# Keeping the conv blocks and silu(z) in HBM, with a lag of 20 blocks, new instruction orders, and the layer norms' squares on ScalarE

## What is computed

```
xz = x @ W_in                      # 256 -> 2 x 512: x_proj, z
x_conv = silu(conv4(x_proj) + conv_b)          # causal, 4 taps, per channel
ssm = x_conv @ W_xproj                         # 33 columns: delta, B (16), C (16)
h_mean = einsum('bld,bln->bdn', x_conv, softplus(delta) * B) / L     # over the whole sequence
y = einsum('bdn,bln->bld', h_mean, C) + D * x_conv
x = layernorm(x + (y * silu(z)) @ W_out)
gate, up = fp4_linear(x, w_gate), fp4_linear(x, w_up)                # 256 -> 704 each
x = layernorm(x + fp4_linear(silu(gate) * up, w_down))               # 704 -> 256
```

## Time and profile before

| | |
|---|---|
| median of three executions | 2203.39 us |
| the profiled execution: its own time | 2204.03 us |
| span of its trace, first to last instruction | 2202.1 us |
| mean granted TensorE clock | 0.98 |
| TensorE busy | 1990.6 us, 90% |
| VectorE busy | 1756.7 us, 80% |
| ScalarE busy | 1111.5 us, 50% |
| GpSimd busy | 1115.6 us, 51% |
| DMA | 90.53 MB, mean 41 GB/s |

### The profile page before, as it was taken

How to read it: one execution, slowest core, us unless ns; L and a number is a source line. 1 busy time by engine, 2 the same in 40 slices (tenths; PEclk the granted TensorE clock), 3 DMA queues, 4 the chain that set the end, 5 groups by cost and what they waited for, 6 DMA issues and landing times.

```text
span 2202.1 us, 37847 instructions
## 1 busy us (share of the span) xinstructions
PE 1990.6 (90%) x10532; PEld 1583.8 (72%) x10532; DVE 1756.7 (80%) x3548; ACT 1111.5 (50%) x2100; POOL 1115.6 (51%) x1643
## 2 busy tenths in 40 slices
PE   1887899899999999899999999899999999877776
PEld 1655688688877888688877888688876888666665
DVE  6234788798978888789877888798887888788875
ACT  2665455555545555455544556455544555423332
POOL 2223455466545556455644555465554556445543
PEclk9999999999999999999999999999999999999998
DMA  2111111111111111111111111111111111000000
GB/s 79 50 56 43 34 49 44 44 43 45 49 41 34 44 48 45 36 49 49 41 38 41 44 44 48 38 49 44 39 41 39 49 45 35 29 20 25 20 20 15
DMA packets 77089, 90.53 MB, mean 41 GB/s; under 512 B 8881, under 2 KB 59953, under 8 KB 76849
## 3 DMA queue, kind: packets, MB, share of 16 engines
q1 hardware_dynamic: 76848, 87.73, 12.2%
HBM read 37.37 MB, written 16.78 MB: 25 GB/s over the span
## 4 chain that ended last, share of the span: by engine, by line
PE 76%; issue 5%; DVE 4%; ACT 3%; POOL 1%; ACTq 0%; DVEq 0%; POOLq 0%
PE pgu L489 23%; PE pd L489 14%; PE pd L537 9%; PE pa L489 6%; PE pb L489 6%; PE pc L571 4%; PE pc L519 4%; PE pe_ L631 2%; PE pa L559 2%; PE pc L496 2%; PE pe_ L548 1%; PE pd L638 1%; DVE hbuf L990 1%; DVE qsh L820 1%; PE pa L615 1%
## 5 line engine op out<-in xcount | busy, mean ns | idle before, releaser
L489 PE MATMUL pgu<-wgu_hi,xqT 128*128 128x512 f32 (+1 forms) x1536 | 427.7, 387 | 0.9 <-issue 0.9
L489 PE MATMUL pd<-wd_hi,hqT 128*128 128x256 f32 (+1 forms) x1536 | 334.5, 299 | 18.7 <-DVE r L1012 15.5
L489 PEld LDWEIGHTS pgu<-wgu_hi,xqT 128*128 128x128 f32 x1536 | 279.8, 190 | 75.8 <-issue 27.6
L537 PE MATMUL pd<-wout,g 128*128 128x256 f32 x1024 | 259.9, 398 | 49.6 <-DVE hqT L980 35.2
L489 PEld LDWEIGHTS pd<-wd_hi,hqT 128*128 128x128 f32 (+1 forms) x1536 | 255.8, 190 | 57.4 <-issue 23.8
L946 DVE SCALAR_TENSOR_TENSOR acc<-xps,cw,acc 128x512 f32<-128x512 f32 x256 | 248.7, 972 | 24.4 <-POOL acc L429 23.7
L418 POOL TENSOR_SCALAR rs<-mv 128x1 f32<-128x1 f32 x128 | 61.6, 481 | 396.4 <-DVE mv L1027 228.8
L537 PEld LDWEIGHTS pd<-wout,g 128*128 128x128 f32 x1024 | 191.5, 195 | 79.7 <-issue 56.0
L741 ACT ACTIVATE hqT<-pe_ 128x512 fp32r<-128x512 f32 x128 | 76.2, 595 | 335.3 <-PE pe_ L631 335.3
L402 POOL TENSOR_TENSOR xv<-xnq,qsx 128x256 f32<-128x256 bf16 x128 | 79.5, 621 | 300.1 <-DVE xnq L839 300.1
L489 PE MATMUL pgu<-wgu_lo,xqT 128*128 128x512 f32 (+1 forms) x768 | 228.3, 379 | 0.0
(11 more groups left out here) (132 smaller groups left out, 4669.2 us busy)
## 6 DMA issues: line engine op xcount, KB each, us to landing
xcr<-xcs SPq DMA_DIRECT2D x128, 256.0 KB, 2.3
xin<-in_L_attn_x_dram SPq DMA_DIRECT2D x32, 512.0 KB, 3.9
xres<-in_L_attn_x_dram SPq DMA_DIRECT2D x128, 128.0 KB, 2.1
out_dram<-outb SPq DMA_DIRECT2D x128, 128.0 KB, 1.7
szr<-in_L_attn_W_in_dram SPq DMA_DIRECT2D x1, 1024.0 KB, 7.4
szr<-in_L_ffn_w_down_dram SPq DMA_DIRECT2D x1, 704.0 KB, 8.6
szr<-in_L_ffn_w_gate_dram SPq DMA_DIRECT2D x1, 640.0 KB, 4.5
szr<-in_L_ffn_w_up_dram SPq DMA_DIRECT2D x1, 640.0 KB, 5.7
```

The costliest lines, as they stand in the source:

```text
L489: mm = pe.matmul(bank, lhsT, rhs, start=(m == 0), stop=(m == len(pairs) - 1))
L537: mm = pe.matmul(pd[:, 0:DM], g[:, (s + 1) % 2, c, j * P:(j + 1) * P], wout[:, c, :], start=(c == 0), stop=(c == NB - 1))
```

## The change

- `walk` has one form of block, with a lag of 20 blocks (`LAG` = 5 supers) in place of 16. `late_y`, `tail_here` and `ring_place` are gone.
- `szr` and `xcr` are gone. The conv block goes to HBM (`xc_hbm`), silu(z) through a small buffer `szs` to HBM (`sz_hbm`), and both are loaded again one block ahead of use into `xl` and `zl` (2 buffers each). All of this is on the SP queue. The weights' raw data lies in a scratch tensor.
- The layer norms lose `bn_stats` and `bn_aggr` on VectorE. The residual sums carry an accumulator output (sum of the row), ScalarE computes (sum - 256 x)^2 with an accumulator output, and GpSimd works from those two numbers.
- h is quantised over two blocks (last two steps in the next block), its product goes to a tensor `hq` of its own, and the last third of h's transposes goes to bank `pb` in place of `pd`.
- All four compute engines have new orders inside a block.

The core of the diff (orders of TensorE, VectorE, ScalarE, and the new DMAs and sums):

```
+    LAG = SPS + 1
+    xc_hbm = nc.dram_tensor("xc_hbm", [NT, P, ST], F32)
+    sz_hbm = nc.dram_tensor("sz_hbm", [NT, P, ST], F32)
-        szr = sb("szr", [P, NB, SPS, ST])
-        xcr = sb("xcr", [P, NB, SPS, ST])
+        xl = sb("xl", [P, 2, ST])
+        zl = sb("zl", [P, 2, ST])
+        szs = sb("szs", [P, 2, ST])
...
+        def stages(g, j):
+            u = 4 * g + j
+            w = u - 4 * LAG
+            return u, u - 1, w, w - 4, w - 5, w - 6, w - 7, w - 8
...
                     if exists(to + 1):
                         at_least(q, r_done, to)
                         q.dma_start(xres[:, (j + 1) % 2, :], xtile[to + 1])
+                    if exists(w + 1):
+                        n, half = (j + 1) % 2, 16 * (2 * i + (j + 1) // 2 + 1)
+                        wait_apart(q, (xc_saved[n], half), (sz_saved[n], half), (g_ready, w))
+                        q.dma_start(xl[:, n, :], xc_hbm[w + 1]).then_inc(xl_landed[n], 16)
+                        q.dma_start(zl[:, n, :], sz_hbm[w + 1]).then_inc(zl_landed[n], 16)
...
-                        q.dma_start(xcr[:, jb, sb_, :], xcs[:, jb % 2, :]).then_inc(xc_saved[jb % 2], 16)
+                        q.wait_ge(xc_ready, v + 1)
+                        q.dma_start(xc_hbm[v], xcs[:, (j + 1) % 2, :]).then_inc(xc_saved[(j + 1) % 2], 16)
...
+                        q.wait_ge(z_ready, u + 1)
+                        q.dma_start(sz_hbm[u], szs[:, j % 2, :]).then_inc(sz_saved[j % 2], 16)
...
+            def output_projection(j, s, i, tz):
+                pe.wait_ge(g_ready, 4 * i)
+                at_least(pe, r2_done, capped(tz + 1, NT))
...
+            def state_projection(j, jb, g_, v, w):
+                pe.wait_ge(xc_ready, v + 1)
+                at_least(pe, yd_done, w + 1)
...
+                    if j == 0 and p1:
+                        transposed_input(g_, u, v)
+                    if exists(tg):
                         gate_and_up(tg)
+                    if p1:
+                        x_product(j, g_, u, v)
                     if exists(td):
+                        transposed_h(td, u)
+                    if p2:
+                        y_product(j, s, b, g_, v, w)
+                    if exists(to):
+                        output_projection(j, s, i, tz)
+                    if j == 1 and tail:
+                        partial_state(g_, w)
                     if j != 1 and exists(v):
+                        state_projection(j, jb, g_, v, w)
+                        transposed_conv(jb, u, v)
                     if exists(tx):
                         transposed_x(td, tx)
+                    if p1:
+                        z_product(j, u, td)
+                    if j == 1 and exists(v):
+                        state_projection(j, jb, g_, v, w)
+                        transposed_conv(jb, u, v)
+                    if j == 3 and tail:
+                        transposed_c(g_, v)
                     if exists(td):
                         down_projection(to, td)
...
+            def deviations(summed, n, r, total, ssq, ssq_done):
+                act.wait_ge(summed, n + 1)
+                act.activation(dev[:, :], r, ACT.Square, bias=total[:, :], scale=-1.0 * DM,
+                               accum_out=ssq[:, :]).then_inc(ssq_done, 1)
...
+                    if exists(tz):
+                        dve.wait_ge(dn_pe, tz + 1)
+                        at_least(dve, out_ready, tz)
+                        dve.scalar_tensor_tensor(r2[:, :], pd[:, 0:DM], 1.0, r1[:, j, :], ALU.mult, ALU.add,
+                                                 accum_out=sum2[:, :]).then_inc(r2_done, 1)
                     if j == 0 and p1:
                         for k in range(KM):
+                            dve.wait_ge(xt_h, 2 * g_ + k + 1)
                             dve.tensor_tensor(xt_lo[:, k, :], (pa, pb)[k][:, :], xt_hi[:, k, :],
...
+                    if exists(td):
+                        q_add(h, h_big).then_inc(hq_link, 1)
+                        q_take(h, h_big, hnq[:, :]).then_inc(hq_link, 1)
...
+                    if p2:
+                        dve.wait_ge(y_pe, w + 1)
+                        dve.wait_ge(xl_landed[j % 2], 16 * (2 * i + j // 2 + 1))
+                        at_least(dve, o_pe, 4 * i - 4)
+                        dve.scalar_tensor_tensor(g[:, second(s) % 2, j, :], xl[:, j % 2, :], dsk[:, j:j + 1], pc[:, :],
+                                                 ALU.mult, ALU.add).then_inc(yd_done, 1)
```

633 lines of the change are left out of this document (262 added, 371 removed).

## The result

The changed kernel takes **2676.91 us** (median of four, 2670.66 to 2679.1), the kernel before beside it 2202.06 (2200.66 to 2206.25): 1.2148 times as long, 95% interval 1.2119 to 1.2177. The prediction was 2526 us in a range of 2291 to 2618. Its direction and its closed loop came true, its size did not: 151 us too little, and outside the range. The profiled execution took 2674.74 us, its span is 2672.7 us, the mean clock 0.899 (0.98 before). DMAs moved 191.38 MB (90.53 before).

What follows compares the result with a forecast made beforehand. A loop between VectorE (take-up of down to `y_skip`) and TensorE was to bound each block: 72.3 us per super plus 3.3 for the clock, 75.6; 636 + 25 x 75.6 gave 2526 us, range 2291 to 2618.

Steps and rivals of the forecast that it cites:

- closed loop: Every block: end of down, VectorE to `y_skip`, TensorE from state projection to next down's end; 11.0 plus 5.5 us at j = 2.
- The clock: TensorE's clock falls to its lower level after stalls: two falls per super at 1.65 us each, +3.3 us.
- the edge: Supers at a sequence's edge, beyond the clean 60.04 us: 66 us over 25 supers, removed by the lag of 20.
- The ends: First phase alone 136 us, the end after the full supers 350 us, a tail super staying near 50.8 us.
- The first phase alone: Five supers at 27.2 us, 136 us in all, with 4 x 0.64 us saved per super on silu(z).
- The collision: VectorE's divide of x held beside GpSimd's product of h: 1.0 us in place of 0.56, +0.44 per block.
- Loads at no cost: Two loads per block, issued a block before use: 16 us of lead against 2.3 us to land, cost 0.
- Statistics at no cost: bn_stats and bn_aggr leave VectorE, squares run on ScalarE beside VectorE's quantisation: 0, without that cover up to 1.5 us.
- milder: VectorE's stretch to `y_skip` stays at 10.1 us, no ScalarE detour or clock fall: 69.1 us per super, 2363 us; chance 0.18.
- faster: Wait on `yd_done`: stretch at most 8.2 us keeps TensorE full, 2137 us; gains end at 8.8 us; chance 0.10.
- the same: Nothing changes: VectorE's stretch to `y_skip` is 8.8 us, a super stays near 62.7 us; chance 0.02.
- late loads: `y_skip` stands 2 us for the load of `xl`: 83.6 us per super, 2726 us; chance 0.04, with anything worse.

## Why the prediction was wrong in size

**The closed loop: right.** State projection and partial sums wait on `y_skip` in every block of the full supers; stretch 10.8 us for 11.0, stall 2.4 for 2.8. By the period of a block, j = 2 measured 16.4 us (16.5 predicted). j = 3 took 17.8 (16.95): C's transposes waited for ScalarE's copy, which I had not seen in the queue. All four sum to 73.0 with the clock at full, against 72.3.

**The clock: the step that failed.** It was put as "two falls per super, +3.3 us", with ends of 0 and +6.6. With the stalls filled by idle work a full super is 6.1 us shorter, so 3.3 should have been about 6. Over 25 supers the term is 2.8 x 25 = 70 us of the 149 missing in the span.

The sum behind the 3.3 fits by luck. It took 3.18 + 2.40 us of stalls off the 8.9 us by which the super from 888.28 is longer than a clean one. But the 3.18 us stand ahead of 888.28 and belong to the super before, which is 3.2 us over a clean one for them:

```profile
825.00:888.28 63.28, 59.91 (x329) 48.58 (x329) 55.58 (x114) 34.59 (x66) 38.15 (x56) 1.00 0.14 45
```

Of the 8.9 us, 4.7 are idle time of TensorE (2.40 and shorter stalls), and 4.2 are longer busy time: 64.08 us for 59.87. The clock did fall twice there: it was 0.50 over the 3 us from 888.30 and 0.55 over the 3 us from 921.90. If the 4.2 us are the clock's, as the 0.95 suggests, a fall cost about 2.1 us, not 1.65 (an estimate), and the 6.1 us are some three falls.

The 3.18 us are not an edge of the data either. TensorE stands as long at the end of a sequence in the changed kernel, whose orders are the same in every super (3.22 us at 1330.13, also with nothing to wait for that the trace shows). It does so five times in each kernel, 14.3 us in all before and 12.2 after, each time where the program's loop over the sequences starts its next pass (six passes, five returns). So these 14 us of the 66 that the prediction gave to the edge could not go with the lag. That the return itself costs them is inferred from the place; no run changed the loop.

**The ends: the same failure, where I had not put the term at all.** "A tail super stays near 50.8" left the clock at its 1.00. The rest took 391 us for 350, and 36 of these 41 us went with idle work there. Why its clock fell, when the stalls of a super add up to no more than before (10.1 us in 56, against 11.2 in 51), is open. The 350 was also summed too low: it took the last double super of the kernel before at 69 us, a sequence's first, but that super runs from 1833.96 to 1894.0, 60 us. With 60 the sum is 359, and the miss 33 us. The range failed by this: its upper end took 79.3 us per super, which holds the 79.15 measured, but with ends of 136 and 350 us.

**The first phase alone: a saving that did not come.** I took 0.64 us per block off for silu(z), and had 27.2 us per super; measured 31.2, and 29.9 with idle work and the clock full, what it was before (29.8). The tap's copy comes sooner behind the acc copy, but dB is later at j = 1 (TensorE stands 1.2 to 1.9 us there, 1.0 with idle work, 0.5 before). The miss is 20 us in all, and 13.5 remain with the clock full; dB accounts for a few of them, the rest is open.

**The collision: wrong in place, and right in the sum by luck.** +0.44 on x's divide was +0.99 on x's scale and -0.14 on the divide, 0.85 in all; the two taps, which the sum had at 0.97 each, took 0.76, and their 0.42 paid for the difference.

**Loads at no cost: right**, shown with 3% of the columns moved and by the list of waits, which has no load in it. **Entry of the second phase: right**, 92.7 for 94. **Statistics at no cost:** not tested in the changed kernel; in the kernel before the same edit cost 2.0%, about half of it by a collision.

The budget of the span: weights 0, first phase +20, entry -1, clock of 25 full supers +70, the rest of them +18 (73.0 for 72.3), end +41; together 148 of the 149 us. This takes the 6.1 us of the run with idle work for the clock, and the prediction's own 350 for the end.

The rivals: milder, faster, the same and late loads are all refuted by S = 79.15 and the list of waits. The "faster" rival named the right place, the wait on `yd_done`, but its point does not hold. With h's two steps back the stretch is 8.6 us in a block (1223.01 to 1231.61 of that run), under its 8.8, but TensorE still stands 0.7 to 1.2 us in each block and S is 66.69, not under 62.7. With `y_skip` early the wait was all but gone and S was 69.09, since copies on ScalarE and h's low halves were the next waits. Only with those moved too did the same lag come out at 0.991, and with idle work in the ends.

## What to carry to other kernels

When an order is written out by hand, look for the closed loop that it makes between two in-order queues: the stretch of the one between the instruction that waits for the other and the instruction that the other waits for. Here moving one VectorE instruction out of that stretch was worth 244 us of 2677, while 130 MB less DMA traffic was worth nothing. Once the loop is cut, look for the next wait: here one copy's place on ScalarE was worth 100 us. And where TensorE stands in every block, price its clock in every stage that has the stall, the ends too, and check first that the stall you calibrate on lies inside the stretch whose length you explain.

## What was not expected of the hardware

- Idle matrix work shortens a kernel: 14 transposes of an identity per block took it from 2677 to 2487 us, 5 of them to 2609; the clock of the full supers rose from 0.91 to 1.00 and 0.93.
- A VectorE `tensor_scalar` of 16 columns took 1.22 us in place of 0.18 beside GpSimd's product (128x704), ending within 0.03 us of it. Moved out of the way, it left the wait to the next instruction (0.42 to 1.58 us).
- TensorE stands 1.6 to 3.4 us each time its loop starts a next pass, in both kernels, with nothing to wait for that the trace shows.
- The accumulator's read is an instruction of its own: 83 ns on VectorE, 0.19 us on ScalarE.
